# Layer 0 of a two-layer attention kernel: softmax denominators taken by half as side jobs, and a second bank for side jobs

## The reference

```python
xn = layernorm(x)
qs = (xn @ Wq.T).reshape(b, s, H, 2, F); ks_ = (xn @ Wk.T).reshape(b, s, H, 2, F); vs = (xn @ Wv.T).reshape(b, s, H, DH)
scores = jnp.einsum('bqhif,bkhif->ibhqk', qs, ks_) * scale
atts = jax.nn.softmax(scores, axis=-1)
att = atts[0] - diff_weight * atts[1]
o = jnp.einsum('bhqk,bkhe->bqhe', att, vs)
rms = jax.lax.rsqrt(jnp.mean(o * o, axis=(-2, -1), keepdims=True) + eps)
s = ((o * rms * norm_w).reshape(b, s, e) @ Wo.T + bo) * (1.0 - diff_weight)
g = silu(scaling * einsum('btr,bte,eor->bto', ce, gate, routed))   # gate: top 2 of 8 routes of xn
x = x + s * g
```

## Time and profile before

| | us |
|---|---|
| median of 3 runs | 1203.16 (1201.54 to 1203.2) |
| profiled execution, span | 1204.5 |
| PE busy | 1161.7 (96%) |
| DVE busy | 901.2 (75%) |
| ACT busy | 677.8 (56%) |
| POOL busy | 571.2 (47%) |

### The profile page before, as it was taken

The page is one execution under the profiler, slowest core; times in us unless marked ns, Lnnn a source line. Parts: engine busy times, 40 slices in busy tenths (PEclk is TensorE's granted clock), DMA queues, the critical chain, the costliest instruction groups (busy, mean ns, idle before and its releaser), DMA issues. The chain is left out here.

```text
span 1204.5 us, 34940 instructions
## 1 busy us (share of the span) xinstructions
PE 1161.7 (96%) x14327; PEld 755.9 (63%) x14327; DVE 901.2 (75%) x1993; ACT 677.8 (56%) x1302; POOL 571.2 (47%) x599
## 2 busy tenths in 40 slices
PE   6999999999999999999989999999999999999997
PEld 5433444444444444443368787878879787887976
DVE  6777887868788887878275967778687767768766
ACT  4357676776777677666643544445344444535453
POOL 2156686776868586777622413232231413223131
PEclk8589999999999999999989999999999999999999
DMA  8445254553525345352240010010101001010100
GB/s 236 105 96 135 70 138 119 116 151 79 143 71 136 104 115 132 93 156 72 71 127 1 4 54 3 12 46 4 54 4 54 4 16 41 4 54 4 36 4 19
DMA packets 57998, 86.80 MB, mean 72 GB/s; under 512 B 8304, under 2 KB 38256, under 8 KB 57840
## 3 DMA queue, kind: packets, MB, share of 16 engines
q1 hardware_dynamic: 57680, 84.31, 26.6%
q10 hardware_dynamic: 160, 0.26, 0.1%
HBM read 50.40 MB, written 33.55 MB: 70 GB/s over the span
## 5 line engine op out<-in xcount | busy, mean ns | idle before, releaser
L1111 DVE TENSOR_REDUCE negmax<-s_bank 128x1 f32<-128x512 f32 x512 | 330.2, 679 | 74.3 <-PE s_bank L759 73.7
L1306 POOL TENSOR_TENSOR room<-room 128x512 f32<-128x512 f32 x248 | 310.9, 1286 | 121.7 <-ACT room L925 121.7
L925 ACT ACTIVATE room<-t_bank 128x512 f32<-128x512 f32 x512 | 284.1, 600 | 84.2 <-PE t_bank L769 80.6
L769 PE MATMUL t_bank<-qst,kst 50*128 50x512 f32 x512 | 202.6, 472 | 6.1 <-ACT room L925 5.7
L759 PE MATMUL s_bank<-kst,qst 48*128 48x512 f32 x512 | 195.6, 475 | 5.1 <-DVE negmax L1111 2.9
L769 PEld LDWEIGHTS t_bank<-qst,kst 50*128 50x128 f32 x512 | 82.1, 189 | 102.1 <-ACT room L925 62.2
L2068 POOL TENSOR_TENSOR win<-rt,apart 128x512 f32<-128x512 f32 x32 | 41.9, 1331 | 211.6 <-DVE rt L1874 211.6
L1598 PE MATMUL pr<-xt_h,win_h 128*128 128x512 f32 x256 | 105.9, 414 | 0.0
L2055 POOL TENSOR_TENSOR ex<-ex,rc 128x256 f32<-128x256 f32 x64 | 41.7, 652 | 130.1 <-DVE rc L1902 130.1
L1598 PE MATMUL pr<-xt_l,win_h 128*128 128x512 f32 x256 | 100.5, 393 | 0.0
L1598 PE MATMUL pr<-xt_h,win_l 128*128 128x512 f32 x256 | 100.5, 393 | 0.0
(11 more groups left out here) (333 smaller groups left out, 2576.2 us busy)
## 6 DMA issues: line engine op xcount, KB each, us to landing
park<-qk_h SPq DMA_DIRECT2D x126, 128.0 KB, 2.4
qst<-park SPq DMA_DIRECT2D x64, 192.0 KB, 3.2
kst<-park SPq DMA_DIRECT2D x64, 192.0 KB, 4.2
park<-qk_l SPq DMA_DIRECT2D x64, 128.0 KB, 2.4
room<-in_x SPq DMA_DIRECT2D x8, 512.0 KB, 5.3
xr<-in_x SPq DMA_DIRECT2D x8, 512.0 KB, 6.0
room<-x SPq DMA_DIRECT2D x8, 512.0 KB, 4.0
out<-so SPq DMA_DIRECT2D x32, 128.0 KB, 1.7
```

The source lines that it names most:

```text
L769: pe.matmul(t_bank[w % 2][:, :], kst[slot][rows, j, c * P:(c + 1) * P], qst[slot][rows, j, :], start=True, stop=True).then_inc(m.t_done, 1)
L925: act.activation(probs[:, c, j, :], t_bank[w % 2][:, :], ACT.Exp, scale=SCALE0).then_inc(m.exp_done, 1)
L1111: dve.tensor_reduce(negmax[:, i_par, 2 * odd + j, c:c + 1], s_bank[n % S_BANKS][:, :], X, ALU.max, negate=True).then_inc(m.max_done, 1)
L1306: add = pool.tensor_tensor(sums[:, pair, h, :], probs[:, 2 * pair, h, :], probs[:, 2 * pair + 1, h, :], ALU.add)
```

## The change

`d_bank` is renamed `spare`, and is free for side jobs. The denominators of a half become one side job, SUM: both of its pairs of sums one after the other, in slots (0, 7), (1, 9), (2, 9) and (3, 9). ACT copies the first half's result into `dt`; for the three others DVE adds the bank to `dt`. Each job now names its slot, its bank, and by how many units ACT and DVE read it later. A slot can hold two jobs, one to each bank: 26 jobs in 26 slots become 26 jobs (and 4 SUM) in 17 slots (and 4). The value steps of half 0 move to the units 3, 5, 11 and 15, the copies of `a_bank` to other units, and DVE's small gate steps, the squares, the statistics and POOL's list are put in another order. In the last batch the denominators of the last half go straight from `probs` into `spare`.

```diff
-DVE_LATER = (("PROJ", 0), ("WF", 0), ("WF", 1), ("WF", 2), ("WF", 3), ("XT", 1))
-ACT_LATER = (("XT", 1),)
+JOBS = (          # slot, kind, shift, k, ACT later, DVE later, bank (0 misc, 1 spare)
+    ((0, 1), "V", 0, 2, 0, 3, 1),
+    ((0, 1), "V", 0, 3, 0, 1, 0),
...
+    ((3, 5), "WF", -1, 3, 0, 0, 1),
+    ((3, 5), "PROJ", 7, 0, 0, 1, 0),
+    ((3, 7), "M", 4, 0, 0, 1, 1),
+    ((3, 7), "V", 1, 0, 0, 0, 0),
...
+VALUES = ((3, 5, 11, 15), (3, 7, 11, 15), (3, 7, 11, 15), (3, 7, 11, 15))
+POOL_ORDER = (("add", -1, 1), ("add", 0, 0), ("add", 0, 1), ("maps",), ("add", 1, 0),
+              ("rms",), ("add", 1, 1), ("residual", 0), ("rstd",), ("add", 2, 0),
+              ("gated",), ("residual", 1), ("add", 2, 1), ("residual", 2), ("add", 3, 0),
+              ("residual", 3))
+SQUARES = ((1, 9), (1, 15), (1, 15), (2, 1))
-SQUARES = ((1, 9), (1, 11), (1, 15), (2, 1))
-SUM_STEPS, EVAC_STEPS, DEVAC = (1, 7), (9, 8, 8, 8), (0, 11)
+EVAC_STEPS = (7, 9, 9, 9)
...
-            def denominators(b, hf, pair):
...
+            def denominators(i, bank):
+
+                for pair in range(PAIRS):
+                    pe.wait_ge(m.sum_ok, PAIRS * i + pair + 1)
+                    for h in range(HG):
+                        mm = pe.matmul(bank[BLK * h:BLK * h + BLK, :], pick[:, i % HALF, :], sums[:, pair, h, :],
+                                       start=(pair == 0), stop=(pair == PAIRS - 1))
+                    mm.then_inc(m.d_done, 1)
+
+            prev = [None, None]
+
+            def side(kind, i, k, n):
+                if prev[n] is not None:
+                    wait(pe, *drained(*prev[n]))
+                if kind == "SUM":
+                    denominators(i, side_banks[n])
+                else:
+                    job(kind, i, i % HALF if kind == "PROJ" else k, side_banks[n])
+                prev[n] = (kind, i, 0 if kind in ("PROJ", "M") else k)
...
+                if kind == "SUM" and i % HALF == 0:
+                    act.wait_ge(m.d_done, PAIRS * (i + 1))
+                    wait(act, m.td_psum, i // HALF)
+                    act.activation(dt_[:, :], bank[:, :], ACT.Copy).then_inc(m.d_evac, 1)
...
+                if kind == "SUM" and i % HALF:
+                    dve.wait_ge(m.d_done, PAIRS * (i + 1))
+                    dve.wait_ge(m.d_evac, i)
+                    dve.tensor_tensor(dt_[:, :], bank[:, :], dt_[:, :], ALU.add).then_inc(m.d_evac, 1)
...
+            side("SUM", HALF * B - 1, 0, spare)
             for kind, i, k in [("TD", B - 1, 0)] + [("TA", B - 1, t) for t in range(QT)]:
```

More of the change, by code:

```diff
@@ L135, in layer0_jobs @@
     jobs = []
-    for slot, (kind, shift, k) in zip(SLOTS, JOBS):
-        by_half = kind in ("PROJ", "M")
+    for slot, kind, shift, k, act_later, dve_later, bank in JOBS:
+        by_half = kind in ("PROJ", "M", "SUM")
         if (shift < 0 and not prv) or (shift >= (4 if by_half else 1) and not nxt):
             continue
-        jobs.append((slot, kind, HALF * b + shift if by_half else b + shift, k))
+        kept = not nxt and slot >= (HALF - 1, VALUES[HALF - 1][1])
+        jobs.append((slot, kind, HALF * b + shift if by_half else b + shift, k, act_later, dve_later, 0 if kept else bank))
     return jobs
@@ L872, in body @@
                                 value_step(b - 1, (step + 16) // 4, (step + 16) % 4)
-                            if last and hf == HALF - 1 and w >= 7:
-                                last_denominators(w // 4 - 1)
-                            if last and (hf, w) == (HALF - 1, UNITS - 1):
+                            if last and hf == HALF - 1 and j:
+                                last_denominators(j - 1)
+                            if last and (hf, j) == (HALF - 1, 3):
                                 value_step(b, hf, 2)
[L877 to L882, removed]
-                        for (jh, jw), kind, i, k in jobs:
+                        for (jh, jw), kind, i, k, _, _, n in jobs:
                             if (jh, jw) == (hf, w):
-                                side(kind, i, k)
+                                side(kind, i, k, n)
             over_batches(body)
@@ L889, in _ @@
             value_step(B - 1, HALF - 1, 3)
-            wait(pe, *drained(*prev))
+            for before in prev:
+                wait(pe, *drained(*before))
             pe.wait_ge(m.max_done, B * HALF * UNITS)
@@ L1037, in body @@
                                     side("SQ", b - 1, t)
-                        if (hf, w) == DEVAC and not first:
-                            side("DEV", b - 1, 0)
                         if (hf, w) == GATE_EXP:
@@ L1043, in body @@
                             side(*FIRST_JOBS[-1], first_banks[-1])
-                        for (jh, jw), kind, i, k in jobs:
-                            if (kind, k) in ACT_LATER and (jh, jw + 1) == (hf, w):
-                                side(kind, i, k)
+                        for (jh, jw), kind, i, k, later, _, n in jobs:
+                            if later and UNITS * jh + jw + later == UNITS * hf + w:
+                                side(kind, i, k, side_banks[n])
                         if first and (hf, w) == WO_SPLIT:
@@ L1052, in body @@
                                 shared.high_weights(act, n)
-                        for (jh, jw), kind, i, k in jobs:
-                            if (jh, jw) == (hf, w) and (kind, k) not in ACT_LATER:
-                                side(kind, i, k)
+                        for (jh, jw), kind, i, k, later, _, n in jobs:
+                            if (jh, jw) == (hf, w) and not later:
+                                side(kind, i, k, side_banks[n])
             over_batches(body)
-            side("DEV", B - 1, 0)
             values_out(HALF * B - 1, HALF - 1)
@@ L1242, in body @@
                                 norm_ends(b + 2)
[L1243 to L1245 removed]
+                        for (jh, jw), kind, i, k, _, later, n in jobs:
+                            if UNITS * jh + jw + later == UNITS * hf + w:
+                                side(kind, i, k, side_banks[n])
                         for step in range(len(GATE)):
```

104 lines of the change are left out of this document (52 added, 52 removed), and 17 rows, old and new, of tables (JOBS, SLOTS).

## The result

The changed kernel takes 1224.22 us (median of 4 runs, 1222.62 to 1226.55) against 1203.18 before on the same chip: a ratio of 1.0169, 95% interval 1.0148 to 1.0191. It is slower by 21 us, where +4 was forecast and 1216 was the upper end of the range. The profiled execution has a span of 1220.8 us (before 1204.5) at a mean granted clock of 0.969 (before 0.975).

A forecast was written before the change was run, and what follows sets the result against it. PE's own order was taken to bound layer 0. A middle batch: -1.5 - 1.4 + 0.4 + 1.1 + 2.2 = +0.8 us; with six of them and the edges +4.2, so 1207 us was forecast, range 1190 to 1216.

The forecast's parts named there:

- (e): PE's wait at V in slot (3, 7), through POOL's residual, SP's store and park: +2.2 us per middle batch, bounds 0 and 3.5.
- The third rival: POOL's late list also delays ACT's exponentials, half a microsecond in halves 1 and 3; +2.1 per middle batch, 1215 us; chance 0.15.
- the park's upper value: Upper bound of (e), 3.5 us: the park's issue takes as long as its copies do with full queues.
- (a): Joined jobs on PE spare nine changes of the kind of matmul: -1.5 us per batch, bounds 1.3 and 2.2.
- (b): PE's waits for the one side bank and for ACT's copy of `a_bank` go: -1.4 us per batch, bounds 1.0 and 2.0.
- (c): DVE adds three 128x512 sums per batch, mostly hidden: +0.4 us per batch, bounds 0 and 2.0.
- (d): ACT has more work than PE in slots (1, 13) to (2, 1): +1.1 us per batch, bounds 0 and 1.7.
- the first rival: (e) is not there, as POOL is in time or V's bank free: -1.4 us per middle batch, 1194 us; chance 0.22.

The follow-up runs named there:

- experiment 1: Changed kernel, with SP issuing the store of tile 1 of the batch before behind park 6 instead of ahead of it: 1194.0 us, ratio 0.9919 to before.
- experiment 2: Changed kernel, with 12 unused matmuls ahead of M in slot (3, 7) of batches 1 to 6: 1212.9 us, ratio 1.0072 to before.
- experiment 5: Kernel before, with POOL's residual of tile 1 behind gated instead of behind the first add of half 2: 1220.26 us, ratio 1.0148.
- experiment 3: Changed kernel, with POOL's residual of tile 1 ahead of the first add of half 2: 1206.11 us, ratio 1.0019 to before.
- experiment 6: Kernel of experiment 1, with the second square back in its old slot (1, 11): 1194.11 us, ratio 0.9936.
- experiment 7: Kernel of experiment 1, with DVE's three additions for the running sum taking 8 columns instead of 512: 1194.54 us, ratio 0.9933.
- experiment 11: Kernel of experiment 1, with DVE gate steps on two SBUF operands moved to POOL's idle slots and the second square in (1, 11): 1191.96 us, ratio 0.9898.
- experiment 4: Kernel before, with the store of tile 1 put behind park 6 in SP's queue: 1205.15 us, ratio 1.001.
- experiment 10: Kernel before, with three DVE gate steps moved from slot (1, 4), where POOL is idle, to (1, 8), where it adds: 1215.5 us, ratio 1.0096.
- experiment 8: Kernel of experiment 1, with five of the nine joined jobs standing alone again, each in its own bank: 1228.12 us, ratio 1.0222.

## Why the prediction was wrong

The direction was right, and so was the mechanism of term (e); its size was not.

**(e), predicted 2.2 us per middle batch, measured 5.0 (experiment 1).** This is the step that failed: the wait was sized 0.6 us too short, and the half clock that comes with it was not in the sum at all. The walk itself, counted from PE's first matmul of slot (2, 8) at 453.29 in batch 5:

| step | predicted | measured |
|---|---|---|
| rstd_of begins | 2.2 | 2.4 |
| first add of half 2 begins | 4.1 | 4.3 |
| gated begins | 9.1 | 10.1 |
| residual ended | 11.7 | 12.7 |
| last issue of the park begins | 15.2 | 16.4 |
| park landed | 17.6 | 18.8 |
| ACT writes `qk_h` | 17.6 | 18.9 |
| PE begins V, `qk_l` being ready | 19.0 | 20.3 |
| PE is at V | 16.8 | 17.3 |

The wait came out longer, 2.85 here and 2.75 in the mean. The chain is 1.3 us late, most of it since POOL's gated waited 0.78 us for DVE's last gate step, which the change puts behind the add; PE is late too, by 0.5. The park went as predicted: 3.2 us from its first to its last issue (466.50 to 469.68), and 2.4 from there to its landing (472.06). The Trainium skill, "DMA: Bandwidth & Descriptors", section "Anatomy of one DMA", has about 2.0 us for the fixed part of this, but of DMAs that GpSimd issues; this one is issued by SP, and 2.4 is what it took.

The other 2.3 us were nowhere in the sum. The prediction priced PE's idle time as idle time alone. With the wait of some 2.8 us the granted clock fell to half for 3.4 or 6.8 us in each of the six batches (0.93 to 0.98 in the mean of a batch, 1.00 in the earlier trace rows), and in batch 1 once more. Experiment 2 gives at least 1.5 us per batch for it. By the prices of experiment 5 (1.3 us for 3.4, 2.6 to 2.8 for 6.8) the 34 us at half clock in the batches 1 to 6 come to 13 to 14 us, 2.2 to 2.3 per batch: an estimate, and with the 2.75 of the wait it makes up the 5.0. The bound of 3.5 for (e) was too low for that reason. Here, too, the fall does not hang on a long idle time alone. The other fall of batch 1, at 148.7 us, has PE busy ahead of it, with no gap over 0.25 us in 8 us:

```profile
144.00:148.00 4.00, 3.67 (x21) 1.40 (x19) 3.97 (x8) 2.92 (x8) 3.81 (x4) 1.00 0.01 2
149.00:152.00 3.00, 3.00 (x16) 1.21 (x8) 2.42 (x7) 2.15 (x8) 0.00 (x0) 0.50 0.77 177
```

What makes the clock fall there stays open.

The third rival had the right side. Its half microsecond on ACT was there, but shows only with the edit of experiment 3. Its sum is also wrong by its own terms: 0.8, with 1.3 for the park's upper value and 1.0 on ACT, is +3.1 us per batch and not +2.1, and 6 x 3.1 - 0.6 gives 1221 us and not 1215. That would have been near the 1224, by luck, since neither addend is what happened.

**(a) and (b), predicted -2.9 us.** The signs are there in part. WF and PROJ joined take 1.17 + 1.48 us (466.10, 467.27, 468.75), against 1.26 + 1.58 in the earlier trace rows: 0.19 us spared, as taken. XT and TA joined take 1.02 us in experiment 1 against 2 x 0.58, though 0.49 and not 0.44 lie between them. In batch 5 of experiment 1 no matmul waits for its side bank, and only some weight loads still do. The sum can be read from the distances between the starts of PE's matmuls in batch 5. One kind runs from a pair's matmul to another pair's matmul; the rest begin or end at a job, a value step or a sum. The rest adds up to 57.7 us before and 55.6 in experiment 1: -2.2 before rounding, not -2.9. It is (a) and (b) together; how much is either was not tried.

**(c), predicted +0.4, and (d), +1.1.** The distances from pair to pair rise from 11.4 to 12.9 us: +1.4 against +1.5, a fair sum with a wrong content. The square gave nothing back (experiment 6), and shorter sums 0.1 us (experiment 7). What costs is DVE's gate steps. The change moved them beside POOL's adds, and DVE loses 3 us per batch by it (61.2 - 56.2, less the sums' 2). With most of them in POOL's gaps and the square back, DVE is busy for 59.1 us, the distances from pair to pair are 11.7, and 0.9 us per batch return (experiment 11). The prediction's sum does not mention these steps. The last 0.2 us was not taken away by any run.

**The sum of (a) to (d)** was -1.4 us and came out at -0.85 (415.2 to 410.1 over six batches). The edges made up for it. What is ahead of batch 1 was to be -0.9 and is -2.4 in the changed kernel and -1.9 in experiment 1, but batch 0 alone takes from 71.2 us (13.7 of them at half clock, changed kernel) to 75.9 (25.6, experiment 7) with the change in it, so that its part is not known to 2 us. Batch 7 and what follows were to be +0.3 and are -6.0 and -6.2. Three things are in this:

- Batch 7 up to its last exponential takes 60.0 us in the changed kernel and 60.2 in experiment 1, against 62.0 in the experiments 4 and 5, which have the old tables. From there to the first matmul of layer 1 it is 22.5 against 23.5. These 3 us go with the change and were not foreseen; what they come from was not tried.
- Before's own trace has 63.3 us in batch 7, with 3.4 at half clock, and 6.8 at half clock between the layers, where the changed kernel and experiment 4 have 3.4. That is its own execution and nothing of the change.
- Layer 1, which the change leaves alone, took from 568.6 us (experiment 5) to 574.2 (experiment 10) from its first projection to the end.

So the first rival's 1194 is what experiment 1 measured, and that is luck: its gain per batch was 1.4 and is 0.85, and the rest comes from edges that it put at -0.6.

## What to carry to other kernels

When a table that orders one engine is changed, walk every queue that hangs on it up to the next program order: here a residual on POOL held a store, the store held a park behind it in SP's queue, and that held ACT, DVE, a bank and PE, and moving one store took back 30 us. Price an idle stretch of TensorE with what the clock may add to it: here 3.4 us at half clock cost 1.3 us and 6.8 us 2.6 to 2.8, on top of the stretch itself, and it came behind short stretches as well as long ones. And look where small VectorE steps on two SBUF operands stand against GpSimd's work: two such steps put beside its additions cost 1.0 us per batch (experiment 10).

## What was not expected of the hardware

- In otherwise dense matmuls the granted clock fell to 0.50 (1.2 GHz) for 3.4 or 6.8 us at each of the seven gaps of 2.5 to 3.0 us (changed kernel and experiment 5), at three of five gaps of about 1.6 us (experiment 5), and at times with no gap over 0.25 us in the 8 us before (batch 1 of the changed kernel). A dozen matmuls in the gap kept it at 1.00 in all six batches (experiment 2).
- VectorE's steps of 128x4 and 128x32 on two SBUF operands took 0.15 to 0.20 us in GpSimd's idle time, up to 1.3 us beside its additions of 1.25 us, and one 1.78 us beside a GpSimd operation of 2.38 us (experiment 8). TENSOR_REDUCE of one operand, and additions with one operand in PSUM, kept their time. Of the TENSOR_SCALAR steps of 128x4, one in each run took 0.85 to 1.18 us beside an addition instead of 0.15.
